# A six-layer decoder with a routed last layer: four samples' rows scattered from two buffers, the last step's first loads reordered, own rows loaded ahead of the join, sums in pairs

## What is computed

```python
logits = xf @ gate_w + gate_b
probs = jax.nn.softmax(logits, axis=-1)
gates, expert_idx = jax.lax.top_k(probs, K)          # K = 2 of E = 8 experts
h = jax.nn.relu(jnp.einsum('nc,ech->neh', xf, w1) + b1)
expert_out = jnp.einsum('neh,ehc->nec', h, w2) + b2
out = jnp.einsum('ne,nec->nc', weights, expert_out)  # weights: the two gates
x = _layernorm(x + out, axis=-1)
```

## Time and profile before

| what | value |
|---|---|
| timed runs | 996.41 us median of 3 (993.87 to 996.79) |
| profiled execution | 998.28 us, of which 995.2 us are the profiler's span |
| TensorE busy | 868.6 us (87%) |
| VectorE, ScalarE, GpSimd busy | 615.4, 497.9, 297.1 us |
| DMA | 102.33 MB, mean 103 GB/s |

### The profile page before, as it was taken

The page is one execution under the profiler, slowest core; times in us unless marked ns, Lnnn a source line. Parts: engine busy times, 40 slices in busy tenths (PEclk is TensorE's granted clock), DMA queues, the critical chain, the costliest instruction groups (busy, mean ns, idle before and its releaser), DMA issues.

```text
span 995.2 us, 19709 instructions
## 1 busy us (share of the span) xinstructions
PE 868.6 (87%) x7316; PEld 688.7 (69%) x7316; DVE 615.4 (62%) x1840; ACT 497.9 (50%) x1159; POOL 297.1 (30%) x478
## 2 busy tenths in 40 slices
PE   3669899999999899999999999999999999299950
PEld 2446668667777666777678777877877888289940
DVE  4998776676765768866848685778854434200016
ACT  2335446553656454553465545565555555045535
POOL 4423322222343123431213333232421214212236
PEclk9679999999999989999999999999999999689985
DMA  8996000000010000000000030231121226699836
GB/s 323 400 323 210 2 1 12 12 7 17 17 33 28 18 7 17 22 22 17 6 2 22 23 118 23 91 118 54 55 84 54 92 91 212 225 318 351 321 129 235
DMA packets 35950, 102.33 MB, mean 103 GB/s; under 512 B 4984, under 2 KB 20352, under 8 KB 35296
## 3 DMA queue, kind: packets, MB, share of 16 engines
q1 hardware_dynamic: 32448, 91.74, 27.0%
q0 software_dynamic: 3408, 9.34, 2.5%
HBM read 87.53 MB, written 33.35 MB: 121 GB/s over the span
## 4 chain that ended last, share of the span: by engine, by line
PE 63%; DVE 19%; ACT 7%; issue 6%; DMA 3%; POOL 1%; SPq 0%; ACTq 0%; DVEq 0%; POOLq 0%
PE ps L705 44%; PE ps L710 7%; PE ps L717 5%; PE ps L781 3%; DVE PT L1104 2%; DVE stat L1045 2%; ACT PT L1438 2%; ACT slot_rows L1438 1%; PE ps L848 1%; DMA xs_d<-X,idx 1%; PE ps L1006 1%; DVE sm L1061 1%; DVE PT L1069 1%; DMA KB<-xs_d 1%; DVE stat L1046 1%
## 5 line engine op out<-in xcount | busy, mean ns | idle before, releaser
L1626 POOL TENSOR_TENSOR stat<-stat,mhalf 128x1 f32<-128x1 f32 x112 | 67.1, 599 | 291.2 <-DVE stat L1047 291.1
L705 PE MATMUL ps<-wall,slot_rows 128*128 128x256 f32 (+1 forms) x448 | 132.3, 424 | 11.3 <-ACT KB L1465 8.9
L705 PEld LDWEIGHTS ps<-wall,slot_rows 128*128 128x128 f32 x448 | 79.1, 193 | 36.0 <-issue 22.8
L710 PE MATMUL ps<-cst,PT 128*128 128x128 f32 x512 | 73.4, 280 | 14.9 <-DVE PT L1104 4.2
L717 PE MATMUL ps<-KB 32*128 32x128 f32 (+1 forms) x2048 | 76.9, 287 | 7.2 <-DVE PT L1104 2.4
L1104 DVE TENSOR_REDUCE PT<-ps 128x8 f32<-128x1024 f32 x64 | 75.3, 1219 | 12.5 <-PE ps L717 12.4
L705 PE MATMUL ps<-wgu,slot_rows 128*128 128x352 f32 x256 | 82.1, 473 | 0.8 <-ACT slot_rows L1400 0.6
L717 PEld LDWEIGHTS ps<-KB 32*128 32x128 f32 (+1 forms) x2048 | 64.9, 190 | 25.7 <-issue 20.6
L705 PEld LDWEIGHTS ps<-slot_rows,wall 128*128 128x128 f32 x640 | 75.8, 193 | 8.5 <-issue 4.1
L705 PE MATMUL ps<-slot_rows,wall 128*128 128x128 f32 x640 | 79.6, 279 | 1.8 <-DVE KB L1165 0.9
L710 PEld LDWEIGHTS ps<-cst,PT 128*128 128x128 f32 x512 | 58.7, 143 | 30.6 <-issue 16.2
(11 more groups left out here) (237 smaller groups left out, 1817.5 us busy)
## 6 DMA issues: line engine op xcount, KB each, us to landing
EW<-moe_w SPq DMA_DIRECT2D x23, 514.0 KB, 4.3
EW<-moe_w SPq DMA_DIRECT2D x23, 512.0 KB, 5.0
PT<-moe_w SPq DMA_DIRECT2D x12, 514.0 KB, 5.9
PT<-moe_w SPq DMA_DIRECT2D x12, 512.0 KB, 6.9
wall<-wts SPq DMA_DIRECT2D x1, 4104.0 KB, 20.4
...
```

The source lines that it names most:

```text
L705: last = k.e.matmul(o, a, b, start=(i == 0), stop=(i == len(pairs) - 1))
L710: last = k.e.transpose(ps[:, u.at, c * P:(c + 1) * P], src[:, c * P:(c + 1) * P], ident)
L1626: return k.e.tensor_tensor(v[:, 7:8], v[:, 8:9], mhalf[:, :], ALU.pow)
```

## The change

Four edits. Late samples: for samples 12 to 15 (`TWIN`) ScalarE copies the rows to a second buffer (`twin_rows`, in slot 4's rows), GpSimd writes its destination and gate, and both scatters are issued one behind the other; `pool_second` is left with samples 0 to 11. Early loads: they go tile by tile, rows first, then up, then down; before, all weights went first and the rows behind them. Own rows: they are saved to a DRAM tensor of their own, and loaded back in four DMAs of 512 KB whose place in SyncE's list the planner chooses from when tiles 23, 26, 29 and 32 are stored; the fetches at the end shrink to 256 KB. Join: ten groups of one or two samples share the additions, the small statistics operations and the root, and in groups 2, 5 and 9 VectorE does both additions. The planner's costs and pieces are changed to match.

```diff
+GROUPS = [range(0, 1), range(1, 3), range(3, 5), range(5, 7), range(7, 9), range(9, 11), range(11, 12), range(12, 14),
+          range(14, 15), range(15, 16)]
+
+BOTH = {2, 5, 9}
...
+OWN = 4
+OWN_AT = [NT - 16 + 3 * i for i in range(B // OWN)]
+
+TWIN = range(B - 4, B)
+DONE = range(B - 6, B - 4)
...
 def plan_router():
     for n in range(B):
-        yield piece(0.25, [(n, "x6T")], [("A", 0.36, (n, "x6T"))], [(n, "done", 1)], True)
+        twin = n in TWIN
+        yield piece(0.25, [(n, "x6T")], [("A", 0.36, (n, "x6T")), ("p", 0.2 + 0.2 * twin, None), *[("a", 0.5, None)] * twin],
+                    [(n, "done", 1), *[(m, "done", 1) for m in DONE] * twin], True)
...
-        yield piece(work=[("D", 2.05, (n, "routed"))], needs=[("f", n - 2, "gT")] * (n > 1))
-        yield piece(0.4, [(n, "rank")], [("D", 0.78, (n, "rank")), ("P", 1.16, None), ("Q", 0.5, None),
-                                         ("L", 2.4, (n, "half sent"))])
+        yield piece(work=[("D", 2.05, (n, "routed")), *[("p", 0.2, None)] * twin], needs=[("f", n - 2, "gT")] * (n > 1))
+        yield piece(0.4, [(n, "rank")], [("D", 0.78, (n, "rank")), ("P", 1.0, None), ("Q", 0.5, None),
+                                         ("L", 2.4, (n, "half sent"))] if n not in TWIN else
+                    [("D", 0.78, (n, "rank")), ("P", 1.9, None), ("Q", 0.5, None), ("L", 2.6, (n, "sent"))])
...
 def plan_second():
-    for n in range(B):
+    for n in range(TWIN[0]):
...
 def early_turns():
 
-    for kinds in (("load up", "load down"), ("rows",)):
-        yield from ((what, x) for x in range(NT) for what in kinds if early(what, x))
+    yield from ((what, x) for x in range(NT) for what in ("rows", "load up", "load down") if early(what, x))
...
 def join_turns():
 
 
+    yield from (("own", i) for i in range(B // OWN))
     yield from (("fetch", n) for n in range(B))
+    last = len(GROUPS) - 1
     yield "add", 0
-    for n in range(B):
-        if n < B - 1:
-            yield "add", n + 1
-        yield "join", n
-        if n:
-            yield "finish", n - 1
-    yield "finish", B - 1
+    for g in range(last + 1):
+        if g < last:
+            yield "add", g + 1
+        yield "join", g
+        if g:
+            yield "finish", g - 1
+    yield "finish", last
...
-        ys_d = nc.dram_tensor("ys_d", (8 * P + 3 * P * B, D), F32, kind="Internal").ap()
+        ys_d = nc.dram_tensor("ys_d", (8 * P + 2 * P * B, D), F32, kind="Internal").ap()
+        own_d = nc.dram_tensor("own_d", (B * P, D), F32, kind="Internal").ap()
...
+        rows_flat = slot_rows[:, :, :, :].rearrange("p s a b -> p (s a b)")
+        own_rows = rows_flat[:, 0:B * D].rearrange("p (n d) -> p n d", d=D)
...
+        def twin_rows(n):
+
+            lo = (NS - 2) * 5 * D + (n - TWIN[0]) * XW
+            return slot_rows[:, :, :, :].rearrange("p s a b -> p (s a b)")[:, lo:lo + XW]
...
-            lo = 8 * P + 3 * P * n
-            return ys_d[lo:lo + 3 * P, :].rearrange("(p k) d -> p (k d)", k=3)
+            lo = 8 * P + 2 * P * n
+            return ys_d[lo:lo + 2 * P, :].rearrange("(p k) d -> p (k d)", k=2)
...
-            for what, n in join_turns():
+            for what, g in join_turns():
                 if what == "join":
-                    v, rows_ = mv2[:, n % 8, :], join_rows(n)
-                    x6 = rows_[:, 2 * D:3 * D]
-                    k.wait_ge(halved, n + 1)
...
-                    e.tensor_tensor(x6, x6, rows_[:, D:2 * D], ALU.add).then_inc(joined, 1)
-                    k.wait_ge(joined, n + 1)
-                    k.after(k.step(e.bn_stats(v[:, 0:6], x6)))
-                    k.after(k.step(e.bn_aggr(v[:, 6:8], v[:, 0:6])))
-                    e.tensor_scalar(v[:, 8:9], v[:, 7:8], 1e-5, None, ALU.add).then_inc(var6, 1)
-                    e.tensor_scalar(v[:, 6:7], v[:, 6:7], -1.0, None, ALU.mult).then_inc(var6, 1)
+                    n, (y1, y2, x6) = GROUPS[g], joined_rows(g)
+                    v = mv2[:, n[0]:n[-1] + 1, :]
+                    if g in BOTH:
+                        k.wait_ge(own_fetched, 16 * (B // OWN))
+                        for i in n:
+                            k.wait_ge(fetched[i], 16)
+                        k.after(k.step(e.tensor_tensor(x6, x6, y1, ALU.add)))
+                    else:
+                        k.wait_ge(halved, sum(h not in BOTH for h in range(g + 1)))
+                    e.tensor_tensor(x6, x6, y2, ALU.add).then_inc(joined, 1)
+                    k.wait_ge(joined, g + 1)
+                    for i in range(len(n)):
+                        stats = k.step(e.bn_stats(v[:, i, 0:6], x6[:, i, :]))
+                    k.after(stats)
+                    for i in range(len(n)):
+                        aggr = k.step(e.bn_aggr(v[:, i, 6:8], v[:, i, 0:6]))
+                    k.after(aggr)
+                    e.tensor_scalar(v[:, :, 8:9], v[:, :, 7:8], 1e-5, None, ALU.add).then_inc(var6, 1)
+                    e.tensor_scalar(v[:, :, 6:7], v[:, :, 6:7], -1.0, None, ALU.mult).then_inc(var6, 1)
...
         def act_router(k):
             for n in range(B):
                 act_copy(k, U[n]["x6T"], x6T[:, :, :])
+                if n in TWIN:
+                    k.wait_ge(vector[slot(n)], count(VECTOR, n, "normed", 6))
+                    for m in DONE:
+                        k.wait_ge(vector[slot(m)], count(VECTOR, m, "normed", 6))
+                    k.e.copy(twin_rows(n)[:, 0:D], X6[:, slot(n), 0:D]).then_inc(twinned, 1)
...
+        def pool_scatter(k, n, i, rows_):
+            k.e.indirect_dma_start(xs_d, bass.IndirectOffsetOnAxis(ap=idx[:, n, i:i + 1], axis=0), rows_,
+                                   None).then_inc(scattered[slot(n)], 16)
+
         def pool_router(k):
             for n in range(B):
-                yield
-                yield
-                yield
-                k.wait_ge(zeroed, 16 * len(zero_parts))
-                k.wait_ge(idx_ready, n + 1)
                 if n >= NS:
                     k.wait_ge(scattered[slot(n)], sent(n - NS))
                 k.e.tensor_copy(X6[:, slot(n), D:D + 1], k_("dest")[:, 2 * n:2 * n + 1]).then_inc(directed, 1)
+                if n in TWIN:
+                    for m in DONE:
+                        k.wait_ge(vector[slot(m)], count(VECTOR, m, "normed", 6))
+                    k.e.tensor_copy(twin_rows(n)[:, D:D + 1], k_("dest")[:, 2 * n + 1:2 * n + 2]).then_inc(twin_tail, 1)
+                yield
+                yield
+                if n in TWIN:
+                    k.wait_ge(picked, 2 * n + 1)
+                    k.e.tensor_copy(twin_rows(n)[:, D + 1:XW], mx8[:, n, 1:2]).then_inc(twin_tail, 1)
+                yield
+                k.wait_ge(zeroed, 16 * len(zero_parts))
                 k.wait_ge(directed, n + 1)
-                k.e.indirect_dma_start(xs_d, bass.IndirectOffsetOnAxis(ap=idx[:, n, 0:1], axis=0), X6[:, slot(n), :],
-                                       None).then_inc(scattered[slot(n)], 16)
+                k.wait_ge(idx_ready, n + 1)
+                pool_scatter(k, n, 0, X6[:, slot(n), :])
+                if n in TWIN:
+                    k.wait_ge(twinned, n - TWIN[0] + 1)
+                    k.wait_ge(twin_tail, 2 * (n - TWIN[0]) + 2)
+                    pool_scatter(k, n, 1, twin_rows(n))
...
         def pool_second(k):
-            for n in range(B):
+            for n in range(TWIN[0]):
...
         def pool_join(k):
-            for what, n in join_turns():
-                if what == "add":
-                    rows_ = join_rows(n)
-                    x6 = rows_[:, 2 * D:3 * D]
-                    k.wait_ge(fetched[n], 16)
-                    k.e.tensor_tensor(x6, x6, rows_[:, 0:D], ALU.add).then_inc(halved, 1)
+            for what, g in join_turns():
+                if what == "add" and g not in BOTH:
+                    y1, y2, x6 = joined_rows(g)
+                    k.wait_ge(own_fetched, 16 * (B // OWN))
+                    for n in GROUPS[g]:
+                        k.wait_ge(fetched[n], 16)
+                    k.e.tensor_tensor(x6, x6, y1, ALU.add).then_inc(halved, 1)
                 elif what == "join":
-                    k.wait_ge(var6, 2 * n + 2)
-                    pool_root(k, mv2[:, n % 8, :]).then_inc(root6, 1)
+                    n = GROUPS[g]
+                    v = mv2[:, n[0]:n[-1] + 1, :]
+                    k.wait_ge(var6, 2 * g + 2)
+                    k.e.tensor_tensor(v[:, :, 7], v[:, :, 8], bc(mhalf[:, :], len(n)) if len(n) > 1 else mhalf[:, :],
+                                      ALU.pow).then_inc(root6, 1)
...
                 yield
                 u = U[n]["b2"]
                 k.wait_ge(emptied[u.at], u.out)
-                k.e.dma_start(token_rows(n)[:, 2 * D:3 * D], X6[:, slot(n), 0:D]).then_inc(saved[slot(n)], 16)
+                k.e.dma_start(rows_of(own_d, n), X6[:, slot(n), 0:D]).then_inc(saved[slot(n)], 16)
...
         def sp_join(k):
-            for what, n in join_turns():
```

(17 more changed lines are left out.)

66 lines of the change are left out of this document (37 added, 29 removed).

## The result

| | before | after |
|---|---|---|
| median of the timed runs | 995.58 us (992.72 to 996.79, 5 runs) | 1002.19 us (1000.87 to 1005.09, 5 runs) |
| ratio | | 1.0077, 95% interval 1.006 to 1.0095: slower, clear of noise, by under 1% |
| span of the profiled execution | 995.2 us | 1000.2 us |

What follows compares the result with a forecast made beforehand. The prediction took TensorE as the bound until 838.8 us, then a 19 us hole, the tile stage and the join. Its terms -15.4 + 1 - 3.0 + 2 = -15.4 us gave 982.0 us, range 976 to 989.

Steps and rivals of the forecast that it cites:

- The samples' reordering: Samples' stages up to 838.8 us: reordered lists open or close a few TensorE gaps, +2 us, bounds -4 and +6.
- Three halves: Step 1's tail: one up and two downs move behind sample 15's ranks, which then come 5.3 us earlier.
- The filler is missed: Rival: TensorE idles before sample 15's last layer, so its ranks come no earlier; 986 us, chance 0.13.
- Slower: Rival: reordering opens TensorE gaps between 100 and 838.8 us, 33.7 growing past 51; chance 0.03.
- behind the layer: From the end of sample 15's last layer to the last step's first up: 10.1 us shorter.
- Scatters, table: After sample 15's ranks: scatters issued about 1 us apart at 848 to 849, table ready at 851.8.
- The rows are there before: Start of the last step: rows land before the first up's weights, so the first up starts at 858.8, 15.4 us earlier.
- the landing that I had reckoned: First up's weights: a 514 KB load issued at 854.5 lands in 4.2 us, at 858.7.
- The DMA as next bound: Rival: in the tile stage TensorE waits for loads; 984 to 986 us, chance 0.12.
- The size of the term: Tile stage: own rows and earlier start shrink the loads' 13 us in hand to 2.4, costing 1 us.
- The join: End of the kernel: paired joins save 2.7 us and smaller fetches 0.3, together 3.0 us less.
- the wide addition: Join: a 512-column addition on VectorE takes 0.69 us, 0.84 at most.

Runs made afterwards that it cites:

- rows_all_first: The changed kernel with the three early row loads issued ahead of all weights; 1005.41 us, ratio 1.0103.
- weights_first: old_order_twin with the early loads in their former order, all weights of four tiles and then the rows; 995.49 us, ratio 1.0001.
- single_no_twin: single_joins without the second buffer, so all 16 samples copy their rows' tail between the two scatters; 993.16 us, ratio 0.9981.
- old_order_twin: The changed kernel with the planner's two former assumed costs for samples 0 to 11; 991.63 us, ratio 0.9966.
- single_joins: old_order_twin with sixteen join groups of one sample and no group with both additions on VectorE; 990.68 us, ratio 0.9944.
- join_only: The kernel before with only the change's own rows and join, TensorE's list as before; 995.73 us, ratio 1.0.
- reorder_only: The kernel before with two assumed planner costs changed (router piece, scatter), no instruction added or removed; 1008.09 us, ratio 1.012.
- order_root_cost: The kernel before with one planner number changed, a 0.2 us GpSimd cost for each sample's first router piece; 1029.51 us, ratio 1.0336.

## Why the prediction was wrong

**Where the bound lies.** Right: TensorE in the samples, a hole, a full tile stage, a join. The sizes were off in each but the tile stage, and by far the most in the first.

**The samples' reordering: the step that failed.** "I take +2 (bounds -4 and +6)", and the tail's "Three halves: 5.3 us", which "holds only if TensorE stays full until 838.8". Together -3.3 us; measured +11.0, 14.3 us off. The gaps grew by 12.6 us instead of 2 (46.3 against 33.7), and TensorE's work there did not shrink by 5.3 but by 1.5 us, though three halves had left. Of the 3.8 us that are missing, an estimated 3 are the clock: some 6 us more at half clock than before, in which work takes twice as long. That was not tried by itself. The ranks ended at 864.0, not 847.0. Behind the bounds stood no row at all: "Two or three such gaps more or less" was a feeling. The runs put the spread for one changed number at -3 to +34 us.

**The halves themselves.** Between the layer's end and the ranks stand six halves before and after, and this took 14.1 and 14.2 us. The gain could come only from the layer ending earlier, that is, from the very stretch in which the gaps grew. "The filler is missed" and "Slower" were kept as two rivals with a price each, 4 and over 17 us; here they came together. Slower was said to decide at 51 us of gaps; it decided at 46.3, because the other gains came smaller too (1.5 of 5.3 us from the halves, 5.3 of 10.1 behind the layer, 1.1 of 3.0 in the join).

**Scatters, table.** Right: the two scatters of sample 15 were issued 1.27 us apart (865.76, 867.03), before the table ended at 868.97, 5.0 us behind the ranks (4.8 predicted); the first load of rows went out 1.6 us later, as said.

**The first up.** From the ranks to the first up 11.8 us were predicted, 15.9 measured, 21.3 before. The step "The rows are there before" is true of the first tile and not of the second, which TensorE's list wants as well before the first up. It costs some 4 us against the landing that I had reckoned (the up's weights, issued at 871.68, would by 4.2 us have landed at 875.9; the up started at 879.88); rows_all_first shows that only 0.9 of it comes back by putting all rows ahead. The stretch was still 5.4 us shorter than before. In the old order the traces give its parts, from the ranks to the first up: 21.3 us before, 21.0 with the second buffer alone (weights_first), 16.35 with tile by tile alone (single_no_twin), 14.0 with both (old_order_twin; 14.1 in single_joins). The second buffer gains 0.3 us while the rows stand behind all weights, and 2.2 once they do not. Why the changed kernel, with both, needs 15.9 and not 14.0 is seen as far as the second tile's rows: they took 6.1 us, in old_order_twin 3.8; the cause of that is open.

**The DMA as next bound.** Rightly kept a rival: 84.6 us at a DMA share of 0.89 and 339 GB/s, against 85 to 87 with 0.97 expected; TensorE is busy for 83.65 of 84.58 us. The size of the term was off to the safe side:

```profile
879.88:950.00 70.12, 69.19 (x478) 64.58 (x478) 3.19 (x20) 35.60 (x126) 16.10 (x17) 0.98 1.03 391
```

The engines are full up to 950 us at 391 GB/s, where I had reckoned with a share of 0.95. The loads took some 79 us from the first rows' issue on instead of 85.5, and TensorE reached the last down at 962.57, so some 12 us stayed in hand, not 2.4. The Trainium skill, "DMA: Bandwidth & Descriptors", section "Bandwidth", gives some 358 GB/s for a core when both cores of its HBM domain stream, and measured 425 with one core alone. One core ran here, and the trace agrees with the second: 391 GB/s over 70 us is above 358 and under 425. The stage's 339 are lower because its last 14 us have little to load. The prediction took the 358 without that condition.

**The join.** The size was off: 1.1 us instead of 3.0 in the trace of the change, and nothing in the medians (join_only 1.0, single_joins not slower), so that the mechanism is seen in VectorE's stretch alone. Of the sum, the wide addition (0.69) was right; VectorE's stretch was 21.7 instead of 19.6 us. Missed was that a pair starts only when two fetches and a 1.26 us addition are done, and that a root of two columns is no cheaper than 0.8 to 1.1 us.

**The account.** reorder_only +12.5 and old_order_twin -4.0 us add up to +8.5; the change measured +6.6. The two are within the spread of medians and of the order of the tail, which both change.

**Open.** That the order costs the time is shown; why an order is good or bad was not settled. The runs show which waits grow (TensorE on ScalarE's results, and in order_root_cost on VectorE's) and that bad orders have more table loads on ScalarE, 61 and 65 against 57 and 58. A run that keeps TensorE's order and changes only the number of table loads would tell how much they hold; there is none. That the clock falls with the waits is read from a few places, and how much of the 11 us it holds was not tried by itself.
